# A grouped convolution's column shifts stacked in 96 partitions, and the last chunk's denominators summed by matmul

## The reference

```python
x = x + conv3x3(gn(x), W)            # 32 groups of 4 channels, SAME padding, no bias
x = x + neighbourhood_attention(gn(x), w_qkv, b_qkv, rpb, w_proj, b_proj)
```

## Time and profile before

| what | value |
|---|---|
| time, median of three runs | 1097.95 us |
| time of the profiled execution | 1098.98 us |
| span of its trace | 1097.2 us |
| convolution stage, first to last tap of it | 23.4 to 259.4 us |
| attention stage, first score to last weighing | 260.1 to 1065.0 us |
| tail, to the end of the span | 1065.0 to 1097.2 us |

### The profile page before, as it was taken

How to read it: one execution, slowest core, us unless ns; L and a number is a source line. 1 busy time by engine, 2 the same in 40 slices (tenths; PEclk the granted TensorE clock), 3 DMA queues, 4 the chain that set the end, 5 groups by cost and what they waited for, 6 DMA issues and landing times.

```text
span 1097.2 us, 41269 instructions
## 1 busy us (share of the span) xinstructions
PE 988.8 (90%) x16485; PEld 684.8 (62%) x16485; DVE 810.7 (74%) x2111; ACT 642.0 (59%) x1808; POOL 484.6 (44%) x839
## 2 busy tenths in 40 slices
PE   4999999998999989899998999898999999999882
PEld 3666665564676666666676666666666666666651
DVE  3387774544888787879888888978798788878760
ACT  2111124003786868587877767785868677777561
POOL 5000103203654646374646556474756464555530
PEclk9999999998999989899999999998999899999895
DMA  9321002234467555555746576655657375646311
GB/s 254 91 89 45 31 16 104 92 87 147 131 159 212 150 162 157 161 164 152 218 119 196 145 206 168 166 165 161 173 138 221 95 214 136 204 114 195 97 48 57
DMA packets 122582, 154.73 MB, mean 141 GB/s; under 512 B 30832, under 2 KB 107024, under 8 KB 119064
## 3 DMA queue, kind: packets, MB, share of 16 engines
q1 hardware_dynamic: 121112, 148.20, 48.1%
q0 software_dynamic: 992, 3.90, 1.2%
...
## 4 chain that ended last, share of the span: by engine, by line
PE 68%; DVE 10%; ACT 9%; issue 8%; DMA 3%; ACTq 1%; SPq 1%; POOL 0%; POOLq 0%; DVEq 0%
PE PS L1313 16%; PE PS L1380 13%; PE PS L1419 10%; PE PS L1403 8%; PE PS L1325 6%; PE PS L1396 6%; PE PS L1362 5%; ACT area L805 3%; DVE area L1142 3%; DVE S L1163 3%; ACT S L897 3%; DVE masked L1174 2%; PE PS L1342 2%; DMA bqkv<-b_qkv 2%; PE PS L1429 1%
## 5 line engine op out<-in xcount | busy, mean ns | idle before, releaser
L687 POOL TENSOR_TENSOR late<-masked 128x48 f32<-128x48 f32 (+1 forms) x512 | 153.3, 300 | 368.3 <-DVE masked L1174 356.1
L897 ACT ACTIVATE S<-S 128x384 f32<-128x384 f32 (+1 forms) x512 | 283.0, 555 | 24.1 <-DVE S L1163 21.1
L1163 DVE TENSOR_TENSOR S<-PS,bias 128x384 f32<-128x384 f32 (+1 forms) x512 | 282.5, 552 | 2.9 <-PE PS L1380 0.2
L1380 PE MATMUL PS<-area 97*128 97x48 bf16 (+1 forms) x4096 | 249.9, 207 | 36.4 <-DVE S L1163 32.8
L1153 DVE TENSOR_REDUCE mcol<-PS 128x6 bf16<-128x480 f32 (+2 forms) x288 | 176.1, 612 | 124.5 <-PE PS L1403 124.4
L890 ACT ACTIVATE VT<-PS 128x128 f32<-128x128 f32 x448 | 132.5, 296 | 183.5 <-PE PS L1362 179.5
L1380 PEld LDWEIGHTS PS<-area 97*128 97x128 bf16 x4096 | 178.6, 102 | 83.1 <-DVE S L1163 41.3
L1419 PE MATMUL PS<-S,VT 128*18 128x48 f32 x8192 | 196.4, 214 | 12.1 <-issue 11.5
L1313 PE MATMUL PS<-padded,wconv 128*128 128x392 f32 x576 | 204.2, 503 | 3.3 <-DVE wconv L1199 3.3
L1419 PEld LDWEIGHTS PS<-S,VT 128*18 128x18 f32 x8192 | 117.1, 99 | 135.3 <-issue 69.5
L1403 PEld LDWEIGHTS PS<-area 128*128 128x128 bf16 x1568 | 144.9, 156 | 22.2 <-issue 7.4
...
## 6 DMA issues: line engine op xcount, KB each, us to landing
area<-k_parts SPq DMA_DIRECT2D x32, 1008.0 KB, 7.1
...
late<-x_mid SPq DMA_DIRECT2D x18, 392.0 KB, 4.9
out<-area SPq DMA_DIRECT2D x18, 392.0 KB, 4.1
den<-sums SPq DMA_DIRECT2D x132, 49.0 KB
```

Of the source, the lines that this page charges most:

```text
L687: nc.gpsimd.tensor_tensor(sel[:, c % SEL_RING, :, :, t0:t0 + count], m[:, :, 0], m[:, :, 1], ALU.add).then_inc(s["summed"], 1)
L897: nc.scalar.activation(S[:, n % 4, 0:cols], S[:, n % 4, 0:cols], ACT.Exp).then_inc(s["probs"], 1)
L1163: nc.vector.tensor_tensor(S[:, n % 4, 0:cols], PS[:, SCORE + n % 2, 0:cols], bias[:, at:at + cols], ALU.add).then_inc(s["biased"], 1)
L1380: last = mm(PS[:, SCORE + n % 2, cols * g:cols * (g + 1)], key_rows[a][0:PEAK_ROW + 1, g, key:key + 128], query_rows[a][0:PEAK_ROW + 1, :, ...
```

## The change

Image 0 keeps the nine-tap form. For images 1 to 15 the three column shifts of a quarter of the channels are copied from `padded`, by three DMAs of 32 partitions, into one tile of 96 partitions; four such tiles serve the four quarters. A slot then has three steps (rows of the kernel) of four matmuls, each with 96 rows of contraction (3 shifts x 32 channels), 32 output channels and 392 columns, in place of the nine matmuls. The weights for it are loaded by nine more DMAs on POOL's queue and masked by three DVE multiplications. The 12 copies of an image are issued half by SP and half by ACT at the top of every even slot. Tiles of the copies lie in space that is free at the time, so some memsets on POOL move, with waits on the convolution. SP's store of the middle image moves by a slot and no longer waits for its own landing. At the end, the denominators of chunk 31 are summed and spread by a matmul with a 0/1 matrix (`sum_rows`), their reciprocals are taken from PSUM, and the last residual is added by DVE from `xa`; in the last chunk `invert` stands in tile 8 instead of 14.

```diff
+    head_of_row = np.where(p % 32 < GROUP_DIMS, p % 32 // HEAD_DIM, 0)
+    c[:, C_SUM:C_SUM + 128] = p[:, None] == (p // 32 * 32 + GROUP_DIMS + head_of_row)[None]
...
+        FIRST_LATE = 10
+        COPY, SPAN = PAD * PAD, PAD * PAD - 2
+        free = ((7520, 7520 + COPY, 7520 + 2 * COPY, 4744), (0, COPY, 2 * COPY, 5824))
+        early = [[part(1, at, COPY) for at in free[b]] for b in range(2)]
+        chosen_f32 = chosen[0].bitcast(F32)
+        later = [[late[:, COPY * t:COPY * (t + 1)] for t in range(4)],
+                 [chosen_f32[:, COPY * t:COPY * (t + 1)] for t in range(3)] + [part(0, KP, COPY)]]
+
+        def copies(m):
+            return (early if m < FIRST_LATE else later)[m % 2]
...
+        def copy_image(eng, m, tiles):
+
+            eng.wait_ge(s["padded_ready"], m + 1)
+            if m > 2:
+                eng.wait_ge(s["conv"], 2 * m - 2)
+            if m == FIRST_LATE:
+                eng.wait_ge(s["table_picked"], UNITS)
+            if m == FIRST_LATE + 1:
+                eng.wait_ge(s["x_mid_out"], 16 * 5)
+                eng.wait_ge(s["stats_out"], 2 * 5)
+            for t in tiles:
+                for dc in range(3):
+                    eng.dma_start(copies(m)[t][32 * dc:32 * dc + 32, 0:SPAN], padded[m % 2][32 * t:32 * t + 32, dc:dc + SPAN]
+                                  ).then_inc(s[f"copies_in{m % 2}"], 16)
...
                 sp.wait_ge(s["conv_added"], 2 * m + 2)
+                if m:
+                    sp.wait_ge(s["x_mid_out"], 16 * m)
                 sp.dma_start(x_mid[m], X[:, m, :]).then_inc(s["x_mid_out"], 16)
-                sp.wait_ge(s["x_mid_out"], 16 * (m + 1))
...
             for h in range(SLOTS):
+                if h % 2 == 0 and h // 2 + 1 < IMAGES:
+                    copy_image(sp, h // 2 + 1, range(0, 2))
                 if 2 * X_RING + h < IMAGES:
                     load_image(2 * X_RING + h)
-                if h % 2:
-                    keep_middle(h // 2)
-                if h == 3:
+                if h % 2 == 0 and h:
+                    keep_middle(h // 2 - 1)
+                if h == 4:
+                    sp.wait_ge(s["x_mid_out"], 16)
                     load_next(0)
...
-            sp.wait_ge(s["table_picked"], UNITS)
+            keep_middle(IMAGES - 1)
+            sp.wait_ge(s["conv"], SLOTS)
             load_residual(IMAGES - 2)
             sp.wait_ge(s["xn_ready"], 2)
             load_next(2)
+            sp.wait_ge(s["x_mid_out"], 16 * IMAGES)
             sp.wait_ge(s["spaces"], SPACES)
             wait(sp, "scores", 1)
+            sp.wait_ge(s["sel_ready"], 1)
...
@@ -635,12 +674,7 @@
                     store_reciprocals(c)
                     if i + 1 < IMAGES:
                         store_queries(i + 1, 2)
-            collect_denominators(2 * IMAGES)
-            pack_denominators(2 * IMAGES)
-            store_reciprocals(2 * IMAGES)
-            spread_reciprocals(2 * IMAGES)
             store(IMAGES, IMAGES - 2)
-            load_residual(IMAGES - 1)
...
+            for dc in range(3):
+                for dr in range(3):
+                    pool.dma_start(wstack[32 * dc:32 * dc + 32, dr, :], conv_w[dr, dc].unsqueeze(0).broadcast_to([8, NORM_GROUP, CH])
+                                   ).then_inc(s["wstack_in"], 16)
...
             pool.wait_ge(s["xin_turned"], 2 * IMAGES)
-            for ap in (kf, V[0], V[1]):
+            nc.gpsimd.memset(kf, 0.0).then_inc(s["spaces"], 1)
+            pool.wait_ge(s["conv"], 2 * (FIRST_LATE - 1))
+            for ap in (V[0], V[1]):
                 nc.gpsimd.memset(ap, 0.0).then_inc(s["spaces"], 1)
...
-            pool.wait_ge(s["table_picked"], UNITS)
-            nc.gpsimd.memset(sel[:, 1:SEL_RING, :, :, :], 1.0).then_inc(s["init"], 1)
             clear_query_rows(0, 11)
-            clear_query_rows(1, 15)
             for h in SPREAD_POOL.values():
                 spread_pool(1, h)
+            clear_query_rows(1, 15)
+            pool.wait_ge(s["conv"], SLOTS)
+            nc.gpsimd.memset(sel[:, 1:SEL_RING, :, :, :], 1.0).then_inc(s["sel_ready"], 1)
...
-            for i in range(IMAGES, IMAGES + 2):
-                add_residual(i)
+            add_residual(IMAGES)
...
+                for side in range(2):
+                    if TURN_FROM + h < IMAGES:
+                        keep_input(TURN_FROM + h, side)
+                    if h % 2 == 0 and h // 2 + 1 < IMAGES:
+                        copy_image(act, h // 2 + 1, range(2 + side, 3 + side))
                 if h == 14:
+                    act.wait_ge(s["spaces"], 1)
+                    fill_ones(0, 4)
+                if h == 20:
                     act.wait_ge(s["spaces"], 3)
-                    fill_ones(0, 4)
...
+                if c < 2:
+                    dve.wait_ge(s["sel_ready"], 1)
...
             nc.vector.tensor_tensor(wconv[:, :, :], wconv[:, :, :], group.unsqueeze(1).broadcast_to([128, 9, CH]), ALU.mult
-                                    ).then_inc(s["padded_ready"], 1)
+                                    ).then_inc(s["wconv_ready"], 1)
...
+                if h == 1:
+                    dve.wait_ge(s["wstack_in"], 16 * 9)
+                    for dc in range(3):
+                        rows = slice(32 * dc, 32 * dc + 32)
+                        own = wstack[rows, :, :].rearrange("p r (t o) -> p (r t) o", o=32)
+                        nc.vector.tensor_tensor(own, own, group[rows, rows].unsqueeze(1).broadcast_to([32, 12, 32]), ALU.mult
+                                                ).then_inc(s["wstack_ready"], 1)
...
-                    if n == RECIPROCAL:
+                    if n == (RECIPROCAL if c + 1 < CHUNKS else LAST_RECIPROCAL):
                         invert(c)
...
             for n in range(TILES - 2, TILES):
                 select_heads(CHUNKS - 1, n)
-            divide(2 * IMAGES)
-            invert(2 * IMAGES)
-            divide(2 * IMAGES + 1)
+            divide(CHUNKS)
+            last = sel[:, (CHUNKS - 1) % SEL_RING, :, :, :].rearrange("p g q t -> p (g q t)")
+            for g in range(2):
+                half = slice(CHUNK_Q * g, CHUNK_Q * (g + 1))
+                wait(dve, "normed", CHUNKS + 1)
+                dve.wait_ge(s["last_sums"], g + 1)
+                link(nc.vector.reciprocal(den[:, half], PS[:, SCORE + g, 0:CHUNK_Q]))
+                nc.vector.tensor_tensor(xn[:, half], last[:, half], den[:, half], ALU.mult).then_inc(s["last_normed"], 1)
+            wait(dve, "misc_out", misc_project(CHUNKS + 1) + 1)
+            wait(dve, "xa_in", 16 * IMAGES)
+            nc.vector.tensor_tensor(yo[:, :], yo[:, :], xa[:, :], ALU.add).then_inc(s["residual"], 1)
...
-            def convolve(h, taps):
+            def convolve(h, row):
 
                 m, half = divmod(h, 2)
-                image = padded[m % 2].rearrange("p (r c) -> p r c", c=PAD)
-                if taps[0] == 0:
-                    pe.wait_ge(s["padded_ready"], m + 2 if m > 1 else 3)
+                to, first = PS[:, h % 2, 0:HALF], row + HALF_ROWS * half
+                if row == 0:
+                    if m:
+                        pe.wait_ge(s[f"copies_in{m % 2}"], 192 * ((m + 1) // 2))
+                        pe.wait_ge(s["wstack_ready"], 3)
+                    else:
+                        pe.wait_ge(s["padded_ready"], 1)
+                        pe.wait_ge(s["wconv_ready"], 1)
                     if h > 1:
                         pe.wait_ge(s["conv_added"], h - 1)
-                for tap in taps:
-                    r, c = tap // 3 + HALF_ROWS * half, tap % 3
-                    last = mm(PS[:, h % 2, 0:HALF], wconv[:, tap, :], image[:, r:r + HALF_ROWS, c:c + SIDE],
-                              start=tap == 0, stop=tap == 8)
-                if taps[-1] == 8:
+                if m:
+                    for t in range(4):
+                        image = copies(m)[t][0:96, :].rearrange("p (r c) -> p r c", c=PAD)
+                        last = mm(to[32 * t:32 * t + 32, :], wstack[0:96, row, 32 * t:32 * t + 32],
+                                  image[:, first:first + HALF_ROWS, 0:SIDE], start=row == 0, stop=row == 2)
+                else:
+                    image = padded[m].rearrange("p (r c) -> p r c", c=PAD)
+                    for c in range(3):
+                        last = mm(to, wconv[:, 3 * row + c, :], image[:, first:first + HALF_ROWS, c:c + SIDE],
+                                  start=row + c == 0, stop=row + c == 4)
+                if row == 2:
                     last.then_inc(s["conv"], 1)
...
-                convolve(h, range(0, 2))
+                convolve(h, 0)
                 if peaks:
                     if peaks[0] == 0:
                         pe.wait_ge(s["placed"], len(PATCH_SOURCES))
                     patch_scores(0, peaks[0])
-                convolve(h, range(2, 5))
...
-                convolve(h, range(5, 8))
+                convolve(h, 2)
                 if peaks:
```

(18 more changed lines are left out.)

36 lines of the change are left out of this document (20 added, 16 removed).

## The result

The changed kernel takes **1065.61 us** (median of 4 runs, 1057.66 to 1071.05) where the kernel before takes 1097.93 beside it: a ratio of 0.9704 [0.9664, 0.9744]. It is faster by 32 us; the prediction had 76, and the time lies 9.6 us above the 1056 up to which its range reached. The profiled execution of the changed kernel took 1068.84 us, with a span of 1066.8.

A forecast was written before the change was run, and what follows sets the result against it. PE was taken to bound the convolution stage, with a chain of waits at the end. 1098.98 less 67.4 (convolution) less 9.0 (tail) is 1022.6; the median, 1.0 lower, 1021.5 us. Own range 1006 to 1034, to 1056 with rival 1.

The forecast's parts named there:

- Four quarters in the time of one: Convolution slots: 24 passes overlap fourfold, as in the weighing, taking 2.0 us a slot, 4.0 less than before.
- Rival 3: Convolution: 392-column passes into different quarters do not overlap, a slot takes 7.9 us for 6.0; 1147 us, chance 0.04.
- the tail: From the last weighing to the end: gain 9 us (6 to 13), including a new 3.0 us DVE wait.
- slots 3 to 16: First convolution stretch: DVE sets the end, 89 us in place of 110, PE alone needing 4.1 us a slot.
- rival 2: Convolution stage: idle PE drops to 1.2 GHz; 25 us more in slots 3 to 16, some 15 elsewhere; 1062 us, chance 0.08.
- The prediction's cover: Time to hide an image's copies: about 9.5 us in slots 3 to 16; in 17 to 31 hidden with nothing to spare.
- slots 17 to 31: Second convolution stretch: 60 us in place of 102, with bounds 47 and 60 + 34.
- 58.0, and 2 us for new round trips: Slots 17 to 31: DVE's 47.3 us busy plus 10.7 waiting for patch scores, plus 2 us, gives 60 us.
- the k_parts row: Copies: profile row of 7.1 us to land 1008 KB, by whose rate an image's 1.38 MB take 9.9 us.
- the dearer row: Copies: profile row giving 0.63 us to issue one DMA, so six issues take 3.8 us.
- that lead: PE being ahead of DVE, expected to cover added waits costed at 2 us; without it ACT's six issues cost 3.8 us.
- Rivals 1 and 2: Rival 1, convolution stage: copies late, at 12 us each, add 34 us; 1055 us, chance 0.20. For the other see rival 2.

The follow-up runs named there:

- the last kernels: Late follow-ups to the changed kernel with grouped steps, SP's queue reordered and short filler matmuls; the final three measured 1056.05, 1050.67 and 1037.27 us.
- ten fillers: Changed kernel plus ten short bf16 matmuls a slot into unused columns, five before the first step and five behind the last: 1058.84 us, ratio 0.9615.
- the second run: The changed kernel, unaltered, run and profiled again: 1068.27 us, ratio 0.9693.
- the last three kernels of the table: Changed kernel with grouped steps, SP reordered, fillers up to slot 16: 1056.05 us; then ACT's copies behind evictions: 1050.67; then copies for four images only: 1037.27.
- few copies: Changed kernel with copies only for images 1, 2, 10 and 11, the others convolved from stale copies: 1048.86 us, ratio 0.9506.

## Why the prediction was right, and where it was wrong

**Right: the matmuls.** Four quarters in the time of one: 24 passes take 2.16 us on the chain of the last kernels at 2.4 GHz, for the 2.0 predicted; by themselves 24 rounds take 16.01 us beside 15.96. At 1.2 GHz they take 4.12 on the same chain, over the 3 us that the prediction named as a sign of being wrong; that is the clock and not the overlap. The estimate of 2.5 us, worked out from the Trainium skill's 2.38 for three column tiles (TensorE: Matmul & The Clock Gate, "Part 3: Packing small matmuls — row/col tiling"), is not borne out. Rival 3, quarters in sequence, is out.

**Right: the tail.** 9 us predicted, 10.8 measured alone, 12.8 in the profiles. DVE and PE in the tail of the changed kernel:

```profile
1039.18 0.47 DVE L1225 RECIPROCAL packed<-packed 128x49 f32<-128x49 f32 x1 [4.18 <-DMA packed<-sums]
...
1048.97 2.52 DVE L1234 TENSOR_TENSOR area<-late,den 128x784 f32<-128x784 f32 x1 [0.51 <-DMA den<-sums]
1051.52 2.61 DVE L1324 RECIPROCAL den<-PS 128x392 f32<-128x392 f32 x1
1054.16 0.57 DVE L1325 TENSOR_TENSOR xn<-late,den 128x392 f32<-128x392 f32 x1
...
1060.09 0.97 DVE L1328 TENSOR_TENSOR yo<-yo,xa 128x784 f32<-128x784 f32 x1 [2.24 <-ACT yo L845]
...
1048.91 1.58 PE L1589 MATMUL PS<-late,sum_rows 128*128 128x392 f32 x4 [0.80 <-POOL late L727]
```

The reciprocals take 2.61 us (2.5 predicted), the product 0.57 (0.55), the new stall of DVE 4.18 (3.0). The last product of the collected kind took 2.52 us where the one of 784 columns at 1084.26 took 0.98; POOL's add of the residual ran beside it. From the last weighing to the end it is 18.7 us for 32.2.

**Wrong: slots 3 to 16.** The step that failed is in rival 2: "at the low level PE is busy all the time and gets the clock back". PE was busy all the time, at the low level, for 126 us from 42.4, and did not get it back. By the prediction's own sum PE then needs 8.2 us a slot, which is the slot of before; it was 7.7, and slots 2 to 15 took 99.8 us instead of 83. Of the 17, at least 12.6 go with the clock: 87.2 us with ten fillers, still 38 of them at 1.2 GHz. The 4 left are that rest and the waits around DVE's own work, and no run parts them. Rival 2's mechanism was right; its chance of 0.08 was the error. That its 1062 in all came close is in part luck: it had 25 us in these slots, where 17 were lost, and 15 in the others, where 27 were. The earlier trace rows show a fall in the attention stage, and the next 4.0 us (349 to 353) ran at 1.00 again; that recovery was carried over to slots made of wide steps, transposes and picks. The clock fell first at 42.4 us, after a stretch in which PE was busy for 4.28 of 6.80 us; the rest of it is the start of a wait of 3.62 us for the first copies. The Trainium skill, TensorE: Matmul & The Clock Gate, "HAM oscillation — how this bites in real kernels", has PE waiting for DMA as the cause; the trace agrees for the first fall, but the low clock went on without waits in the records.

**Wrong: slot 2.** It was to be 4 us shorter, and its add starts 2.1 us later (48.6 for 46.5): 6 us. In the second run of the same kernel it starts at 43.8, so this part comes and goes with the first copies and the fall of the clock. The prediction's cover was worked out for slots 3 to 31 and left image 1 out: its last copy landed 20.8 us after its padding (18.3 in the second run). ACT issued its last three only at 30.9 us, behind the second half of `keep_input`, and the DMA share was 1.05 from 22 to 36 us.

**Wrong: slots 17 to 31.** 66 us from the add of slot 15 to that of slot 31 were predicted, 93.5 measured. The 27 are, by the last three kernels of the table: 11 PE and DVE taking turns, at a clock that was low for 18 us (76.8 without copies, against 66), 7 the copies themselves (84.1 against 76.8), 6 ACT's issues ahead of its evictions (89.9 against 84.1), 4 the rest, in which SP's order and the clock are. Each is a difference of two profiles, good to 3 us at best, and the clock is in each. Copies and ACT's issues together have a second witness: 93.5 against 80.9 with few copies, 12.6 us. The step that failed first is "58.0, and 2 us for new round trips": it took DVE's busy time and its wait for the scores as the length of the slots. The other waits of DVE were hidden before because PE was always late; with PE quick, its next step waits for DVE's add or cast, and DVE for the step, in turn. The prediction counted 2 us for all of them.

**Mis-sized: the copies.** Predicted 6.5 us from padding to landing, bounds 4.2 to 12 (by the rate of the k_parts row 1.38 MB take 9.5 to 9.7, not 9.9). Measured, from the end of the padding to the last landing in the changed kernel: 7.9 to 9.2 us for nine of the 15 images, 10.4 to 14.2 for four, 20.8 for image 1 and 21.3 for image 14. Of it 3.7 to 5.4 us are six issues in one piece (0.5 to 0.87 each, the dearer row had 0.63) and 3.0 to 4.5 the median landings. The prediction named ACT's queue and put it at 3.8 us "where that lead is gone"; the lead was gone. SP's copies "behind stores, fills and moved maxima" were named too; 5.3 us of waiting for `late<-padded` came of it.

**Chances.** Rivals 1 and 2 came together, each in part, and the cases were built as if only one could hold. The two are coupled: a late copy makes PE wait, and the first fall of the clock came in such a wait.
